# A two-layer transformer block on one core: new step orders on five engines, eleven identity products instead of thirty, new bank numbers

## The chip, the core and the metric

The kernel runs on one core of a Trainium2 chip. Five engines work side by side, each through its own list of instructions: TensorE (PE; its weight loads are shown as PEld), VectorE (DVE), ScalarE (ACT), GpSimd (POOL) and SyncE (SP), which issues DMAs. An engine takes its list strictly in order and waits on semaphores. TensorE writes into PSUM banks, VectorE and ScalarE read them, and GpSimd works in SBUF only. The metric is device time in microseconds (us).

## The reference

Two layers work on x (16 sequences of 128 tokens, 128 features) with one conditioning vector per sequence and a context of 120 tokens per sequence. Each layer is self-attention, cross-attention and an MLP, 16 heads of 8 features, all in fp32:

```
# layer 0
x_norm = ln(x) * (1 + scale_a) + shift_a;  q, k, v = x_norm @ W_qkv + b_qkv
x = x + gate_a * (softmax(q k^T * scale) v @ W_proj + b_proj)
x = x + (softmax(q_c k_c^T * scale) v_c) @ W_cproj + b_cproj     # q_c from ln(x), k_c, v_c from ln(context)
x = x + gate_m * (gelu_tanh(modulated ln(x) @ W_mlp1 + b) @ W_mlp2 + b)
# layer 1
x = x + attn(rope(q), rope(k), v) @ sa_out ;  x = x + attn(rope(q), rope(k_ctx), v_ctx) @ ca_out
x = x + gelu(adaln(x) @ ffn_w1 + b) @ ffn_w2 + b
```

## The kernel before, in words

The 16 sequences are four streams of four. A unit f (0 to 15) is one attention of one stream: 0 to 3 is the self-attention of layer 0, 4 to 7 its cross-attention, 8 to 11 the self-attention of layer 1 (with rope), 12 to 15 its cross-attention. m0 to m3 and m4 to m7 are the MLPs. A program is written by hand as five strings of step names, one for each engine (`ORDER`, line 103 on); each step becomes a few instructions, and every wait is derived from the names. Nothing moves at run time: each engine runs its string in order.

The steps of one unit, with the line of the instruction:

- `stats.f` (DVE, L592 and L595), `rstd.f` (POOL, L752 and L755), `ln.f` (DVE, L600): layer norm of the stream. `cstats`, `crstd` and `cln` do it for the context. `xT.f` (PE, L935, then ACT, L866): the transpose and the modulation. `cond`, `mods` and `vec` make the modulation vectors; `warm` is three matmuls on zeros (L975).
- `q.f`, `k.f`, `v.f` (PE, L999 and L1007). `qhi` and `khi` (ACT), `qlo` and `klo` (DVE in layer 0, POOL in layer 1) split each value into a high and a low fp32r part. In layer 1 DVE first multiplies by the cosines and sines (`q.f`, `k.f`, L618) and POOL adds (`qsum`, `ksum`).
- `khmove`, `klmove`, `qhmove`, `qlmove` (SP, L537 and L561, from unit 2 on with a clearing copy, L556): DMAs bring the parts into the row layout Ks and Qd. There are two slots, so a unit's moves wait for the last score step of the unit two before it.
- `max.f.b` (PE, L1025, 16 small matmuls into four banks, then DVE, L690, four reductions): scores of one sequence b, of which only the row maxima are kept. `mT.f.h` (PE, L1038, then ACT, L874) transposes the maxima of two sequences, `mmove.f.h` (SP, L568) brings them into Qd.
- `score.f.b` (PE, L1028, four banks, then ACT, L882, four exponentials), `value.f.b` (PE, L1058, 32 matmuls into the one bank ps_ao), `copy.f.h` (ACT, L889), `norm.f.h` (PE, L1068, then DVE, L699 and L708), `aT.f` (PE, L935, then ACT), `o.f` or `out.f` (PE), `gate` and `yT` where there is a gate, `upd.f` (DVE, L731).

The array is used in three tilings: `max` and `score` use 32 rows of it per matmul, four side by side; `value` uses column groups (18 columns per matmul); everything else the whole array. Counted over the string of PE, the tiling changes 266 times between one step and the next.

All steps but `value` take their PSUM banks from one list of seven banks (`BANK`, one digit per use); a use waits until the reader of the bank's last use has signalled (`fill`). `BESIDE` gives some steps products of the identity with itself, written into the step's own bank between that wait and the step's other wait (`keep_going`, L930).

## Time and profile before

| | us |
|---|---|
| three runs | 380.84, 383.75, 387.33 |
| median | 383.75 |
| the profiled execution | 385.06 |
| its span, first to last instruction | 383.3 |
| TensorE busy | 363.0 |
| VectorE busy | 301.7 |
| ScalarE busy | 254.5 |
| GpSimd busy | 100.6 |

### The profile page before, as it was taken

How to read it: one execution, taken by the hardware profiler on the slowest of the kernel's cores; microseconds unless marked ns; L12 is line 12 of the kernel's file. 1: busy time of each engine (PE TensorE's matmuls, PEld its weight loads, DVE VectorE, ACT ScalarE, POOL GpSimd, SP SyncE). 2: the span in 40 equal slices, each digit the busy share in tenths (PEclk: the TensorE clock that was granted, in tenths of full speed). 3: DMA queues.
4: the chain of work that ended last, by engine and by line, in shares of the span. 5: the costliest groups of instructions: out<-in, count | busy, mean ns of one | idle time of the engine just before them, and what ended most of it. 6: DMA issues, size and time to landing. Idle time of an engine off the chain costs nothing.

```text
span 383.3 us, 12514 instructions
## 1 busy us (share of the span) xinstructions
PE 363.0 (95%) x5090; PEld 260.6 (68%) x5090; DVE 301.7 (79%) x809; ACT 254.5 (66%) x513; POOL 100.6 (26%) x120
## 2 busy tenths in 40 slices
PE   7699999999999999999999999999999899999996
PEld 3485687677776776657654567666677577886776
DVE  5985989999999998947999839997799747875302
ACT  2525965578676987889453797378766945688551
POOL 6920310142020201125351234343413401031130
PEclk9966999999999999999999999999999957999999
DMA  8673244005221360014050140403140404000003
GB/s 208 259 240 93 78 140 167 9 27 186 84 88 43 127 219 5 3 32 169 2 193 6 29 168 7 169 5 106 65 168 4 168 8 159 8 3 3 2 0 111
DMA packets 19757, 34.13 MB, mean 89 GB/s; under 512 B 2740, under 2 KB 7988, under 8 KB 19700
## 3 DMA queue, kind: packets, MB, share of 16 engines
q1 hardware_dynamic: 19268, 33.24, 25.2%
q8 instruction: 41, 0.67, 0.7%
q10 hardware_dynamic: 432, 0.09, 0.2%
q14 instruction: 16, 0.13, 0.1%
HBM read 6.51 MB, written 1.05 MB: 20 GB/s over the span
## 4 chain that ended last, share of the span: by engine, by line
PE 55%; DVE 4%; ACT 3%; DMA 3%; SPq 3%; issue 2%; ACTq 0%; DVEq 0%
PE ps_ao L1058 11%; PE ps_misc L999 8%; PE ps_misc L1028 6%; PE ps_misc L1109 6%; PE ps_misc L1087 6%; PE ps_misc L1025 6%; PE ps_misc L935 3%; PE ps_misc L1094 3%; DVE maxima L690 3%; PE ps_misc L1068 2%; PE ps_misc L1007 2%; ACT PT L882 2%; DMA Ks<-Kl 2%; DMA Ks<-Kh 1%; SPq L537 1%
## 5 line engine op out<-in xcount | busy, mean ns | idle before, releaser
L690 DVE TENSOR_REDUCE maxima<-ps_misc 128x4 f32<-128x512 f32 (+1 forms) x256 | 153.5, 664 | 17.6 <-PE ps_misc L1025 17.1
L882 ACT ACTIVATE PT<-ps_misc 128x512 f32<-128x512 f32 (+1 forms) x256 | 131.7, 606 | 24.0 <-PE ps_misc L1028 22.7
L1058 PE MATMUL ps_ao<-PT,V 120*18 120x128 f32 (+1 forms) x2048 | 70.5, 282 | 0.5 <-ACT PT L882 0.5
L1025 PEld LDWEIGHTS ps_misc<-Ks,Qd 32*128 32x128 f32 x1024 | 41.9, 197 | 30.8 <-issue 11.3
L1025 PE MATMUL ps_misc<-Ks,Qd 32*128 32x128 f32 (+1 forms) x1024 | 53.4, 298 | 8.5 <-DMA Ks<-Kl 3.3
L1058 PEld LDWEIGHTS ps_ao<-PT,V 120*18 120x18 f32 (+1 forms) x2048 | 52.6, 101 | 7.4 <-issue 2.3
L1028 PEld LDWEIGHTS ps_misc<-Qd,Ks 32*128 32x128 f32 (+1 forms) x1024 | 38.0, 186 | 21.5 <-issue 13.7
L752 POOL TENSOR_SCALAR vareps<-mv 128x4 f32<-128x4 f32 (+1 forms) x28 | 6.4, 228 | 170.9 <-DVE mv L595 170.6
L1028 PE MATMUL ps_misc<-Qd,Ks 32*128 32x128 f32 (+1 forms) x1024 | 48.7, 287 | 1.5 <-DVE maxima L690 0.8
L866 ACT ACTIVATE xnT<-ps_misc,vec 128x128 f32<-128x128 f32 x80 | 30.1, 462 | 15.6 <-PE ps_misc L935 15.5
L999 PE MATMUL ps_misc<-xnT,Wr 128*128 128x512 f32 x72 | 37.5, 641 | 1.8 <-ACT xnT L866 1.6
L889 ACT ACTIVATE AOs<-ps_ao 128x512 f32<-128x512 f32 x32 | 19.3, 603 | 26.1 <-PE ps_ao L1058 26.1
L731 DVE TENSOR_TENSOR x<-ps_misc,x 128x512 f32<-128x512 f32 x24 | 16.3, 684 | 23.8 <-PE ps_misc L1109 22.8
L786 POOL TENSOR_TENSOR ropeA<-ropeA,ropeB 128x512 f32<-128x512 f32 (+1 forms) x16 | 20.0, 1257 | 50.6 <-DVE ropeB L618 50.6
L600 DVE TENSOR_SCALAR xn<-x,mv,rstd 128x128 f32<-128x128 f32 x96 | 28.3, 363 | 5.4 <-POOL rstd L755 5.4
L1087 PE MATMUL ps_misc<-xnT,W 128*128 128x512 f32 x64 | 31.1, 603 | 0.2
L755 POOL TENSOR_TENSOR rstd<-vareps,minus_half 128x4 f32<-128x4 f32 (+1 forms) x28 | 29.0, 1037 | 2.3
L911 ACT ACTIVATE hT<-ps_misc,bias 128x512 f32<-128x512 f32 x32 | 20.7, 695 | 12.1 <-PE ps_misc L1087 7.7
L592 DVE BATCH_NORM_STATS2 stats<-x 128x6 f32<-128x128 f32 x96 | 20.8, 279 | 2.9 <-DMA x<-x_in 2.4
L999 PEld LDWEIGHTS ps_misc<-xnT,Wr 128*128 128x128 f32 x72 | 12.6, 197 | 12.1 <-issue 6.5
L1068 PE MATMUL ps_misc<-cst,AOs 128*128 128x128 f32 x128 | 19.5, 280 | 1.3 <-ACT AOs L889 1.1
L1068 PEld LDWEIGHTS ps_misc<-cst,AOs 128*128 128x128 f32 x128 | 15.1, 144 | 5.9 <-issue 3.0
...
## 6 DMA issues: line engine op xcount, KB each, us to landing
...
```

Source lines behind the costliest of these rows:

```text
L600: dve.tensor_scalar(dst[0:rows, b, :], src[0:rows, b, :], mv[0:rows, which, s, b, 0:1], rstd[0:rows, which, s, b:b + 1], ALU.subtract, ALU ...
L690: dve.tensor_reduce(maxima[:, h, st.b % HB, c, :], bank(use + c)[:, 0:NG * ns].rearrange("p (n k) -> p n k", n=NG), AX_X, ALU.max, negate= ...
L755: pool.tensor_tensor(rstd[0:rows, which, st.s, :], vareps[0:rows, which, st.s, :], minus_half[0:rows, :], ALU.pow).then_inc(S["rstd_ready" ...
L866: act.activation(dst[:, b * P:(b + 1) * P], src[:, b * P:(b + 1) * P], ACT.Identity, scale=vec[:, c, mult:mult + 1], bias=vec[:, c, shift: ...
L882: act.activation(PT[0:ns, k % PSLOTS, c, :, :].rearrange("p n t -> p (n t)"), bank(use + c)[0:ns, :], ACT.Exp, scale=SCALE).then_inc(S["pr ...
L999: pe.matmul(bank(st.use + i)[:, 0:n], w_rows(f"{st.kind}{st.a}{form}"), src[:, 0:n], start=True, stop=True).then_inc(S["misc_filled"], 1)
L1025: ins = pe.matmul(bank(st.use + c)[:, n * ns:(n + 1) * ns], queries, keys, start=True, stop=True)
L1028: ins = pe.matmul(bank(st.use + c)[0:ns, n * P:(n + 1) * P], keys, queries, start=True, stop=True)
L1058: last = pe.matmul(ps_ao[32 * c:32 * c + PAIR, block * P:(block + 1) * P], heads[:, at:at + PAIR], PT[0:ns, k % PSLOTS, c, n, :], start=no ...
L1068: last = pe.transpose(bank(st.use)[:, b * P:(b + 1) * P], AOs[:, k % 2, b * P:(b + 1) * P], ident)
L1087: pe.matmul(bank(st.use), w(f"w1_{st.a}", st.b), src, start=True, stop=True).then_inc(S["misc_filled"], 1)
L1109: last = pe.matmul(bank(st.use)[:, b * D:(b + 1) * D], src[:, b * P:(b + 1) * P], weight, start=(i == 0), stop=(i == len(parts) - 1))
```

## The change

All five strings of `ORDER` and the list `BANK` are replaced. The steps are the same, none is added or dropped; what each step computes is the same. `BESIDE` has 11 entries of one product each instead of 22 entries with 30 products. Counted in the new string of PE, the tiling changes 251 times. The code of `keep_going` can now write more than four copies, and `max` and `score` could take identity products too; neither is used by the new table.

```
 BESIDE = {
-    "xT.0": 3, "xT.1": 1, "xT.2": 1, "xT.3": 1, "mT.0.0": 1, "norm.0.1": 1, "aT.0": 1, "norm.1.1": 1, "aT.1": 1,
-    "o.1": 1, "yT.1": 1, "mT.3.0": 2, "norm.3.1": 2, "aT.3": 1, "norm.8.0": 2, "norm.9.1": 1, "xT.12": 3,
-    "mT.11.0": 1, "mT.12.1": 1, "norm.12.1": 1, "norm.13.0": 1, "aT.13": 2,
+    "xT.3": 1, "mT.0.1": 1, "mT.1.0": 1, "mT.1.1": 1, "norm.2.0": 1, "norm.4.0": 1, "yT.3": 1, "mT.12.0": 1,
+    "mT.12.1": 1, "norm.12.1": 1, "mT.14.1": 1,
 }
 ORDER = {
     "pe": """
-        warm.0 mods.0 xT.0 k.0 q.0 xT.1 mods.1 q.1 k.1 max.0.0 v.0 max.0.1 v.1 max.0.2 xT.2 mT.0.0 xT.3 max.0.3 k.2
+        mods.0 warm.0 xT.0 mods.1 q.0 k.0 xT.1 v.0 xT.2 k.1 q.1 max.0.0 max.0.1 v.1 xT.3 max.0.2 v.2 mT.0.0 k.2
...
                 def keep_going(st):
                     n = BESIDE.get(st.name, 0)
-                    if n:
-                        pe.matmul(bank(st.use)[:, 0:n * P], ident, ident[:, None, :].to_broadcast([P, n, P]),
-                                  start=True, stop=True)
+                    while n:
+                        copies = min(n, CB)
+                        pe.matmul(bank(st.use)[:, 0:copies * P], ident,
+                                  ident[:, None, :].to_broadcast([P, copies, P]), start=True, stop=True)
+                        n -= copies
...
                     elif st.kind in ("max", "score"):
                         ns = ns_of(st)
+                        taken = st.name in BESIDE
+                        if taken:
+                            for c in range(HG):
+                                fill(st.use + c)
+                            keep_going(st)
...
-                                if n == 0:
+                                if n == 0 and not taken:
                                     fill(st.use + c)
```

First place: VectorE at the start of the program, before the change, from the statistics of the first stream (`stats.0`) to the second normalisation (`ln.1`).

```order
L592 BN_STATS stats<-x 128x6 x4
L595 BN_AGGR mv<-stats 128x2 x4
L655 TENSOR_SCALAR silu<-silu 128x16
L657 RECIPROCAL silu<-silu 128x16
L659 TENSOR_TENSOR silu<-hT,silu 128x16
L600 TENSOR_SCALAR xn<-x,mv,rstd 128x128 x4
L636 TENSOR_SCALAR vec<-ps_misc,bias 128x16 x2
L592 BN_STATS stats<-x 128x6 x4
L595 BN_AGGR mv<-stats 128x2 x4
L592 BN_STATS stats<-x 128x6 x4
L595 BN_AGGR mv<-stats 128x2 x4
L600 TENSOR_SCALAR xn<-x,mv,rstd 128x128 x4
```

The same place in the change, from the end of `cond`; line numbers are one lower.

```order
L591 BN_STATS stats<-x 128x6 x4
L594 BN_AGGR mv<-stats 128x2 x4
L591 BN_STATS stats<-x 128x6 x4
L594 BN_AGGR mv<-stats 128x2 x4
L635 TENSOR_SCALAR vec<-ps_misc,bias 128x16 x2
L591 BN_STATS stats<-x 128x6 x4
L594 BN_AGGR mv<-stats 128x2 x4
L599 TENSOR_SCALAR xn<-x,mv,rstd 128x128 x4
L591 BN_STATS stats<-x 128x6 x4
L594 BN_AGGR mv<-stats 128x2 x4
L591 BN_STATS stats<-craw 120x6 x4
L594 BN_AGGR mv<-stats 120x2 x4
```

The first normalisation (L600, now L599) stood behind one set of statistics and stands behind three, the third of them on stream 3; two sets of context statistics, which stood behind the first `max` steps of unit 1, follow it.

Second place: TensorE before the change, from `score.12.3` to `max.14.0`, the stretch in which the keys and queries of unit 14 have to arrive (L1028 `score`, L1058 `value`, L1025 `max`, L935 `xT.15`, L1068 `norm.12.0`, L1038 `mT.13.1`, L999 `q.15`).

```order
L1028 MATMUL ps_misc<-Qd,Ks 120x128 x16
L1058 MATMUL ps_ao<-PT,V 18x128 x16
L1025 MATMUL ps_misc<-Ks,Qd 128x120 x16
L935 MATMUL ps_misc<-cst,xn 128x128 x4
L1068 MATMUL ps_misc<-cst,AOs 128x128 x4
L1058 MATMUL ps_ao<-PT,V 18x128 x16
L1028 MATMUL ps_misc<-Qd,Ks 120x128 x16
L1038 MATMUL ps_misc<-cst,maxima 32x128
L999 MATMUL ps_misc<-xnT,Wr 128x512 x2
L1028 MATMUL ps_misc<-Qd,Ks 120x128 x16
L1025 MATMUL ps_misc<-Ks,Qd 128x120 x16
```

The same stretch in the change, from the step behind `score.12.3` on.

```order
L1044 MATMUL ps_misc<-cst,maxima 32x128
L1000 MATMUL ps_misc<-xnT,Wr 128x512 x2
L1031 MATMUL ps_misc<-Ks,Qd 128x120 x16
L936 MATMUL ps_misc<-cst,xn 128x128 x4
L1064 MATMUL ps_ao<-PT,V 18x128 x16
L1031 MATMUL ps_misc<-Ks,Qd 128x120 x16
L1064 MATMUL ps_ao<-PT,V 18x128 x16
L1034 MATMUL ps_misc<-Qd,Ks 120x128 x32
L1044 MATMUL ps_misc<-cst,maxima 32x128
L1074 MATMUL ps_misc<-cst,AOs 128x128 x4
L1000 MATMUL ps_misc<-xnT,Wr 128x512 x2
L1064 MATMUL ps_ao<-PT,V 18x128 x16
```

`q.14`, one more `max`, `mT.13.0` and a third `value` now stand between the two, and two `score` steps follow each other (L1034 x32), so there is one change of tiling less there.

Third place: SyncE in the change, from the last move of unit 14 (`klmove.14`) to the last move of unit 15 (`qlmove.15`).

```order
L536 DMA Ks<-Kl 32x4x480
L567 DMA Qd<-maxT 4x4x128 x2
L536 DMA Ks<-Kl 32x4x480
L555 DMA Qd<-no_shift 4x4x512
L560 DMA Qd<-Qh 32x4x512 x2
L567 DMA Qd<-maxT 4x4x128 x2
L536 DMA Ks<-Kh 32x4x480 x2
L560 DMA Qd<-Ql 32x4x512
```

In the change the maxima of `mmove.14.0` stand inside the moves of unit 15, in front of the two high key moves; before, they stood there too, but behind all three key moves.

## Rows read from the trace of the kernel before

**Rows 1.** The page, its parts 1 and 2: TensorE, and the granted clock in 40 slices.

```profile
PE 363.0 (95%) x5090; PEld 260.6 (68%) x5090; DVE 301.7 (79%) x809; ACT 254.5 (66%) x513; POOL 100.6 (26%) x120
PEclk9966999999999999999999999999999957999999
```

**Rows 2.** Busy time by stretch: start:end, length, engines with instruction counts, granted clock, DMA share, GB/s.

```profile
0.00:19.27 19.27, 13.98 (x52) 8.05 (x52) 14.26 (x65) 7.16 (x14) 14.62 (x20) 1.00 0.74 232
19.27:35.10 15.83, 15.53 (x115) 11.51 (x116) 10.87 (x20) 5.58 (x13) 2.31 (x3) 0.57 0.63 198
35.10:130.54 95.44, 91.10 (x1564) 68.63 (x1560) 88.89 (x240) 68.53 (x139) 16.17 (x28) 1.00 0.27 96
130.54:286.81 156.27, 151.69 (x2116) 102.65 (x2115) 132.51 (x340) 112.41 (x223) 48.70 (x50) 1.00 0.24 83
```

**Rows 3.** The same view around the late stretch of low clock, and one early stretch.

```profile
34.87:48.52 13.65, 12.25 (x210) 8.94 (x214) 12.58 (x39) 11.23 (x23) 3.69 (x8) 1.00 0.21 69
...
294.28:307.93 13.65, 11.23 (x222) 8.30 (x220) 9.96 (x28) 12.27 (x27) 6.25 (x6) 1.00 0.34 119
307.93:321.59 13.66, 13.66 (x205) 10.48 (x209) 8.22 (x16) 5.51 (x11) 1.26 (x1) 0.50 0.20 75
```

**Rows 4.** Timeline of TensorE, value.12.3 to score.13.2: start, length, instructions, [idle before, releaser].

```profile
300.49 1.07 PE L1058 MATMUL ps_ao<-PT,V 120*18 120x128 f32 x32
301.49 0.64 PE L1028 MATMUL ps_misc<-Qd,Ks 32*120 32x128 f32 x16
...
302.18 1.90 PE L999 MATMUL ps_misc<-xnT,Wr 128*128 128x512 f32 x4
304.01 0.70 PE L1028 MATMUL ps_misc<-Qd,Ks 32*120 32x128 f32 x16
306.42 0.67 PE L1025 MATMUL ps_misc<-Ks,Qd 32*128 32x120 f32 x16 [1.71 <-DMA Ks<-Kh]
...
307.86 0.44 PE L1028 MATMUL ps_misc<-Qd,Ks 32*120 32x128 f32 x4 [0.68 <-DVE maxima L690]
```

**Rows 5.** Timeline of TensorE, one value step between others.

```profile
151.04 1.07 PE L1058 MATMUL ps_ao<-PT,V 120*18 120x128 f32 x32
152.04 0.66 PE L1025 MATMUL ps_misc<-Ks,Qd 32*128 32x120 f32 x16
```

**Rows 6.** Timeline of TensorE, two value steps in a row.

```profile
174.44 1.94 PE L1058 MATMUL ps_ao<-PT,V 120*18 120x128 f32 x64
176.31 0.64 PE L1028 MATMUL ps_misc<-Qd,Ks 32*120 32x128 f32 x16
```

**Rows 7.** Timeline of TensorE: mT.12.0, score.11.3 and max.13.0.

```profile
277.59 0.27 PE L1038 MATMUL ps_misc<-cst,maxima 128*32 128x128 f32 x1 [0.38 <-DVE maxima L690]
...
278.77 0.67 PE L1028 MATMUL ps_misc<-Qd,Ks 32*128 32x128 f32 x16
...
286.81 0.66 PE L1025 MATMUL ps_misc<-Ks,Qd 32*128 32x120 f32 x16
```

**Rows 8.** Timeline of SyncE: first and last of unit 13's seven moves.

```profile
279.61 0.55 SPq L556 DMA_DIRECT2D Qd<-no_shift  x1
...
283.03 1.26 SPq L537 DMA_DIRECT2D Ks<-Kh  x2
```

**Rows 9.** Waits of TensorE: who waited for whom: us in total, times, longest.

```profile
PE ps_misc L1068 <- ACT AOs L889: 1.1, 5, 0.3
```

**Rows 10.** Timeline of VectorE at the start: stats.0, ln.0, stats.2.

```profile
3.94 0.87 DVE L592 BATCH_NORM_STATS2 stats<-x 128x6 f32<-128x128 f32 x4 [1.96 <-DMA x<-x_in]
...
6.79 1.29 DVE L600 TENSOR_SCALAR xn<-x,mv,rstd 128x128 f32<-128x128 f32 x4 [1.01 <-POOL rstd L755]
...
10.00 0.87 DVE L592 BATCH_NORM_STATS2 stats<-x 128x6 f32<-128x128 f32 x4 [0.44 <-DMA x<-x_in]
10.90 0.38 DVE L595 BATCH_NORM_AGGREGATE mv<-stats 128x2 f32<-128x6 f32 x4
```

**Rows 11.** Timeline of TensorE: the largest identity product, in front of xT.12.

```profile
248.56 0.91 PE L930 MATMUL ps_misc<-cst 128*128 128x384 f32 x2 [0.15 <-ACT V L849]
```

More of the change, by code:

```diff
@@ L110 @@
-        cT.1 q.4 score.2.2 value.2.1 score.2.3 max.3.3 xT.5 k.5 score.3.0 q.5 norm.2.0 mT.3.1 value.2.2 value.2.3
-        score.3.1 norm.2.1 max.4.0 aT.2 v.5 max.4.1 value.3.0 score.3.2 value.3.1 max.4.2 mT.4.0 score.3.3 o.2
-        max.4.3 value.3.2 score.4.0 yT.2 value.3.3 score.4.1 mT.4.1 norm.3.0 norm.3.1 max.5.0 value.4.0 score.4.2
-        aT.3 max.5.1 value.4.1 score.4.3 o.3 max.5.2 mT.5.0 xT.6 value.4.2 max.5.3 q.6 cT.2 yT.3 value.4.3
-        score.5.0 mT.5.1 norm.4.0 norm.4.1 k.6 v.6 aT.4 score.5.1 value.5.0 score.5.2 cT.3 out.4 k.7 xT.7 max.6.0
@@ L120 @@
-        max.8.2 out.7 h.m2.2 h.m2.0 h.m2.3 max.8.3 h2.m2 mT.8.0 xT.m3 max.9.0 yT.m2 h.m3.3 h.m3.1 max.9.1 mT.8.1
-        h.m3.2 h.m3.0 max.9.2 h2.m3 xT.10 mT.9.0 score.8.0 yT.m3 q.10 k.10 score.8.1 v.10 max.9.3 xT.11 value.8.0
-        score.8.2 value.8.1 score.8.3 mT.9.1 q.11 norm.8.0 score.9.0 value.8.2 score.9.1 k.11 max.10.0 value.8.3
-        score.9.2 norm.8.1 max.10.1 value.9.0 aT.8 max.10.2 value.9.1 score.9.3 norm.9.0 out.8 k.12 max.10.3
-        value.9.2 value.9.3 norm.9.1 max.11.0 v.11 mT.10.0 aT.9 xT.12 max.11.1 mT.10.1 out.9 score.10.0 q.12
@@ L130 @@
-        mT.13.1 q.15 score.13.1 max.14.0 score.13.2 value.13.0 max.14.1 value.13.1 score.13.3 norm.12.1 max.14.2
-        mT.14.0 value.13.2 max.14.3 value.13.3 score.14.0 norm.13.0 score.14.1 mT.14.1 norm.13.1 v.15 max.15.0
-        aT.12 value.14.0 max.15.1 value.14.1 score.14.2 out.12 max.15.2 mT.15.0 score.14.3 aT.13 max.15.3
-        value.14.2 score.15.0 value.14.3 score.15.1 mT.15.1 out.13 xT.m4 norm.14.1 norm.14.0 value.15.0 score.15.2
-        value.15.1 score.15.3 h.m4.2 aT.14 h.m4.3 xT.m5 out.14 norm.15.0 value.15.2 value.15.3 h.m5.0 norm.15.1
@@ new lines @@
+        yT.1 q.4 mT.3.0 score.2.3 value.2.2 max.3.2 cT.1 value.2.3 norm.2.0 max.3.3 v.5 xT.5 score.3.0 q.5 max.4.0
+        mT.3.1 norm.2.1 k.5 score.3.1 value.3.0 aT.2 max.4.1 value.3.1 score.3.2 max.4.2 mT.4.0 cT.2 o.2 score.3.3
+        value.3.2 max.4.3 value.3.3 score.4.0 yT.2 k.6 score.4.1 norm.3.0 v.6 norm.3.1 cT.3 mT.4.1 value.4.0
+        max.5.0 max.5.1 aT.3 value.4.1 o.3 score.4.2 score.4.3 max.5.2 value.4.2 mT.5.0 xT.6 max.5.3 value.4.3 q.6
+        norm.4.1 norm.4.0 score.5.0 mT.5.1 yT.3 aT.4 score.5.1 out.4 value.5.0 score.5.2 score.5.3 value.5.1 k.7
@@ new lines @@
+        xT.7 max.6.0 xT.m0 value.5.2 max.6.1 value.5.3 max.6.2 v.7 norm.5.1 q.7 mT.6.0 h.m0.1 norm.5.0 h.m0.2
+        h.m0.0 aT.5 max.6.3 h.m0.3 out.5 score.6.0 mT.6.1 h2.m0 score.6.1 value.6.0 xT.m1 max.7.0 value.6.1
+        score.6.2 h.m1.2 yT.m0 max.7.1 h.m1.1 h.m1.3 h.m1.0 mT.7.0 max.7.2 value.6.2 score.6.3 h2.m1 xT.8 max.7.3
+        value.6.3 score.7.0 yT.m1 k.8 norm.6.1 mT.7.1 value.7.0 score.7.1 norm.6.0 q.8 aT.6 value.7.1 score.7.2
+        out.6 v.8 xT.9 norm.7.0 value.7.2 score.7.3 k.9 q.9 xT.m2 max.8.0 value.7.3 max.8.1 h.m2.3 norm.7.1 h.m2.1
@@ new lines @@
+        h.m2.2 max.8.2 aT.7 h.m2.0 out.7 v.9 max.8.3 mT.8.0 h2.m2 max.9.0 xT.m3 max.9.1 mT.8.1 h.m3.0 h.m3.3 h.m3.2
+        max.9.2 mT.9.0 h.m3.1 score.8.0 yT.m2 h2.m3 score.8.1 value.8.0 max.9.3 yT.m3 xT.10 value.8.1 score.8.2
+        mT.9.1 q.10 v.10 norm.8.0 score.8.3 k.10 xT.11 value.8.2 value.8.3 score.9.0 score.9.1 q.11 norm.8.1 k.11
+        score.9.2 max.10.0 max.10.1 aT.8 value.9.0 out.8 score.9.3 value.9.1 max.10.2 mT.10.0 v.12 norm.9.0
+        value.9.2 value.9.3 max.10.3 v.11 norm.9.1 k.12 score.10.0 aT.9 max.11.0 mT.10.1 xT.12 out.9 max.11.1
@@ new lines @@
+        value.10.0 score.10.1 k.13 q.12 score.10.2 max.11.2 value.10.1 score.10.3 value.10.2 max.11.3 mT.11.0
+        norm.10.0 xT.13 v.13 value.10.3 mT.11.1 q.13 score.11.0 score.11.1 norm.10.1 k.14 score.11.2 max.12.0
+        value.11.0 max.12.1 value.11.1 aT.10 max.12.2 mT.12.0 out.10 score.11.3 norm.11.0 value.11.2 max.12.3
+        value.11.3 v.14 norm.11.1 k.15 score.12.0 aT.11 xT.14 max.13.0 mT.12.1 out.11 score.12.1 max.13.1
+        value.12.0 score.12.2 value.12.1 score.12.3 mT.13.0 q.14 max.13.2 xT.15 value.12.2 max.13.3 value.12.3
@@ new lines @@
+        score.13.0 score.13.1 mT.13.1 norm.12.0 q.15 value.13.0 max.14.0 score.13.2 max.14.1 value.13.1 score.13.3
+        norm.12.1 max.14.2 mT.14.0 aT.12 value.13.2 max.14.3 value.13.3 score.14.0 norm.13.0 v.15 mT.14.1 max.15.0
+        score.14.1 out.12 max.15.1 value.14.0 score.14.2 norm.13.1 max.15.2 mT.15.0 value.14.1 score.14.3 aT.13
+        value.14.2 max.15.3 value.14.3 score.15.0 score.15.1 mT.15.1 out.13 norm.14.1 xT.m4 norm.14.0 value.15.0
+        value.15.1 score.15.2 score.15.3 aT.14 h.m4.2 xT.m5 out.14 h.m4.0 norm.15.0 value.15.2 value.15.3 h.m4.1
```

142 lines of the change are left out of this document (66 added, 76 removed).

## The prediction

> **What bounds the kernel now.** I read the page first: TensorE is busy 363 of 383 us, so its queue looks like the bound, but the clock row drops below 9 in two places, early and in the slices at about 308 us [rows 1]. Next the stretches. Up to 19.27 us, where the first `max` step starts, VectorE is busy 14.3 us; from there to 35.1 the clock averages 0.57 and VectorE is idle 5.0 us. From 35 to 131 us VectorE is busy 88.9 of 95.4 us (93%), so TensorE partly waits for the maxima it must hand over. From 131 to 287 us TensorE is busy 151.7 of 156.3 us and bounds alone [rows 2]. Then comes a stretch in which TensorE is idle 2.4 us, and behind it 13.7 us at clock 0.50, with TensorE busy all the time [rows 3].
>
> The timeline shows what stood behind that idle time: `max.14.0` waited 1.71 us for a key move, and `score.13.2` stopped 0.68 us in the middle for VectorE's maxima [rows 4]. The same rows give lengths without a wait, from start to start: a value step 1.00 us, a rope query 1.83 us.
>
> I also summed such lengths over all 415 steps, in both orders. Before, TensorE needs about 316 us at full clock; the other 64 us up to its last matmul are waits, start and low clock. A change of order can only reach these 64 us, and the changes of tiling inside the 316.
>
> **The change, part by part.** The steps are the same, so only their places have a price.
>
> *Tiling.* 266 changes become 251, 15 fewer. A value step between steps of other tilings takes 1.00 us [rows 5]; two in a row take 1.87 us, not 2.00 [rows 6]. The one change saved is worth 0.13 us: 15 x 0.13 = **-2.0 us**. All of it lies on TensorE's own queue; where VectorE is the bound it may be lost, so -1.0 to -2.0. The Trainium skill says in TensorEngine Tiling (Array Packing), Key Properties, that switching the tiling mode drains TensorE, and in TensorE: Matmul & The Clock Gate, Step-by-step, that a drain is about 128 cycles; an estimate from these two would be 0.05 us a change at 2.4 GHz and 0.8 us in all. By the rows it is more than twice that, and I go by the rows.
>
> *Moves of keys and queries.* They share two slots, so a unit's seven moves start when the last score of the unit two before is done. For unit 13 that was at 279.44 (278.77 + 0.67), and `max.13.0` started at 286.81: 7.4 us [rows 7]. It is seven issues in 4.68 us, 0.67 each, and 2.5 us from the last issue to the start [rows 8]. Where TensorE has less than 7.4 us of other steps in between, it waits. Summed from step lengths, it had 6.4, 6.1, 6.8 and 7.2 us before units 10 to 13, which makes 1.0 + 1.3 + 0.6 + 0.2, and unit 14 cost the 2.4 us of [rows 4]: 5.5 us together. In the change the same sums are 9.8, 9.8, 10.3 and 7.8 for units 10 to 13: no wait. What is late next are units 14 and 15. For 14, `q.14` now stands directly behind `score.12.3`, and VectorE, GpSimd, ScalarE and SyncE each have a step between it and `max.14.0`; TensorE has 10.1 us behind the score but only 8.1 us behind the query. The price is between 0 and the 2.4 us of [rows 4]; I take 1.5. For 15, the maxima moves of `mmove.14.0` stand inside the seven moves: nine issues, 9 x 0.67 + 2.5 = 8.5 us, against 6.4 us of steps: 2.1 us. Behind `max.15.0` queue `mT.15.0` and with it all of the last unit. Net: -5.5 + 1.5 + 2.1 = **-1.9 us** (bounds -5.5 to +1).
>
> *The late low clock.* 13.66 us at half speed with TensorE busy throughout [rows 3] cost half of that, 6.8 us. In the change the two waits of 1.5 and 2.1 us lie over 10 us apart with steps between them, where before 1.71 and 0.68 us followed within 1.5 us [rows 4]. An early stretch in which TensorE was idle 1.4 us was followed by full clock [rows 3]. I take the fall as gone: **-6.8 us** (bounds -6.8 and 0).
>
> *Waits for copies of the sums.* Five `norm` steps waited for ScalarE's copy, 1.1 us in all [rows 9]: they stood right behind one step after the last value. In the new order every `norm` has at least 0.86 us of steps in front of it: **-1.1 us**.
>
> *Waits for maxima.* `mT.12.0` waited 0.38 us with 2.0 us of steps behind the last `max` [rows 7]. Before, three `mT` steps stood that close (2.03 or less); in the change five do, with 2.03 to 2.12: two more at 0.38, **+0.8 us** (bounds 0 and 2).
>
> *The start.* The first normalisation ran at 6.79 us, after one set of statistics. Now it stands behind `stats.1` and `stats.3`. The third block of x that VectorE took was waited for until 10.00 [rows 10], and stream 3 is loaded about as late, one 240 KB context block earlier; I take its statistics to end at 10.7, so `ln.0` moves 3.9 us. From there to the low part of the first keys VectorE has two sets of statistics of x and of context more than it had (1.28 us each [rows 10]), two more normalisations and the long `vec.1`. Adding its steps gives `klo.0` at about 21 us and the first `max` at 24 to 25 us against 19.27. What comes back: up to `max.2.0`, at 55 us, VectorE has the same list of work in both orders, and before it was idle 5.0 + 5.0 us up to 35.1 [rows 2], waiting for x, then for a slow TensorE. In the new order I count 7.6 us of such idle time up to the first `max`, and little after it, since the work there no longer has to fit between matmuls at half clock. Between 2.4 us gained and the full 4.8 us lost I take **-0.6 us**. On GpSimd, `crstd.2` now waits for context statistics that VectorE does much later, and `rows1` (weights for units 4 to 7) is queued behind it; these are used a stream later, so I put nothing for it.
>
> *Identity products.* 19 fewer; three took 0.91 us [rows 11], about 0.3 each, so 0 to -5.8 us. They stand in front of a wait of their own step, which goes on without them: I take 0.
>
> *Banks.* New numbers move waits between readers; I have no row that prices one by itself, so they sit in the range.
>
> Sum: -2.0 - 1.9 - 6.8 - 1.1 + 0.8 - 0.6 = -11.6 us, from the profiled execution's 385.1 us: **373.5 us**. That execution is 1.3 us above the median of 383.75; the three runs spread from 380.8 to 387.3, so I leave that difference in the range.
>
> **The rivals.**
>
> *The low clock comes back somewhere.* For it: 19 products less are standing in waits between 35 and 131 us, where TensorE's own steps fill little over three quarters of the time by my sums, and units 14 and 15 still wait. Against it: the waits are split. It costs the 6.8 us again: 380.3 us.
>
> *The waits only move.* The first half stays bound by VectorE, whose work there only shrinks by what moved to the start, and in the second half places that were loose have become tight: maxima to transposes from 5.3 to 3.8 us at unit 6, 8.9 to 2.6 at unit 7. The change then does not do what it says, and only tiling is left: 385.1 - 2.0 = 383 us.
>
> *The start is lost and not given back; slower.* The first normalisation waits for stream 3, `max.0.0` starts 4.8 us later, TensorE stands idle in that time, and a second stretch at 0.5 follows the first, in which all units 0 and 1 run at half speed. Price 4.8 + 6.8, with the late fall staying: 385.1 - 2.0 + 11.6 = 394.7 us. It decides if the first `max` starts after 26 us. For it speaks that x arrives when the DMA queue lets it, against it VectorE's 5 us of idle time behind it.
>
> **How the numbers follow.** Forecast 0.50, low clock again 0.24, waits only move 0.16, start lost 0.10. Two per cent of 383.75 is 7.7 us, about what a measurement of this kernel can tell from no change; faster is below 376.1, slower above 391.4. Of the forecast some 0.05 lies above 376.1, since the start alone is uncertain by 5 us; faster 0.45, same 0.05 + 0.24 + 0.16 = 0.45, slower 0.10. The forecast's own range is 368 to 378 (start, banks and identity products). To leave out no more than 0.2 I go up to 387, which takes in the second case and most of the third: 368 to 387.
>
> **What would show it.** Right: one low stretch of the clock, the early one; no key wait before `max.10.0` to `max.13.0`; 1 to 2 us of it before `max.14.0` and `max.15.0`; no `norm` waiting for its copy; the first `max` near 24 us, `max.2.0` near 55 us again. Wrong: clock 0.50 in a second stretch; `max.2.0` after 58 us; VectorE less busy than 93% in the first half; or single long waits for PSUM banks on TensorE that this page does not have.

## The result, and the profile after

The change made the kernel slower: 425.35 us (median of 4 runs, 418.59 to 428.36) against 383.40 us (4 runs, 380.84 to 387.33); the ratio is 1.1012, 95% interval 1.0817 to 1.1207. The medians are over all runs; each ratio in this document is over the faster of two groups into which a kernel's executions fall, here 418.59 and 423.94 us of the four, so it is not the quotient of the medians. The forecast was 373.5 us, the range 368 to 387.

Two numbers of each run split the 42 us: the span and TensorE's mean granted clock. Their product is the span counted in TensorE's granted cycles and written as us at full clock; I call it the **index**. It is not a time, since only TensorE slows with the clock. It moves less between runs of one kernel than the time does: 388.5 to 393.0 in the four runs after, mean 390.4, and 370 to 372 as the mean of the runs of the kernel before in every comparison below. It is not quite free of the clock: it is lowest where the clock is lowest (388.5 at 0.911 and 393.0 at 0.943 after; 367.8 at 0.955 and 374.1 at 0.990 before), so a few us of index between kernels of different clock say little. Some 20 us of the 42 are index, nearly all of it waiting. The clock itself was 0.91 to 0.94 after (mean 0.924) and about 0.97 before: that is the other half.

The page after, parts 1 and 2, against [rows 1]:

```profile
PE 375.9 (90%) x5068; PEld 266.6 (64%) x5068; DVE 304.8 (73%) x809; ACT 254.7 (61%) x513; POOL 100.8 (24%) x120
PEclk9977997999999999999999996996899986989999
```

TensorE is busy 12.9 us more, and it is idle 416.8 - 375.9 = 40.9 us where it was idle 383.3 - 363.0 = 20.3. The other engines do what they did. The clock row has not one dip behind the start but a string of them.

The stretches of [rows 2], cut at the same steps (`max.0.0`, `max.1.0`, `max.6.0`, `max.13.0`); columns as there:

```profile
0.00:23.83 23.83, 13.52 (x58) 8.45 (x58) 18.42 (x83) 8.82 (x19) 18.46 (x24) 1.00 0.59 181
23.83:40.27 16.44, 14.99 (x109) 10.41 (x110) 12.33 (x20) 5.27 (x12) 0.00 (x0) 0.69 0.60 184
40.27:145.97 105.70, 94.47 (x1588) 69.11 (x1587) 86.82 (x232) 69.15 (x140) 16.11 (x28) 0.97 0.25 89
145.97:316.18 170.21, 161.75 (x2074) 108.66 (x2074) 131.64 (x330) 110.32 (x219) 47.79 (x49) 0.95 0.22 76
```

4.6 us are lost up to `max.0.0`, 0.6 in the second stretch, 10.3 in the third and 13.9 in the fourth, which TensorE had filled. VectorE falls from 93% to 82% in the third: it did not become the bound there. What took its place stands in the list of waits. TensorE's waits at `max` (L1025) and `score` (L1028) for ScalarE's exps, and those of its matmul queue (PE) for VectorE's maxima, before (us in total, times, longest):

```profile
PEld ps_misc L1025 <- ACT PT L882: 3.7, 11, 0.8
PEld ps_misc L1028 <- ACT PT L882: 3.0, 8, 0.8
PE ps_misc L1025 <- ACT PT L882: 1.2, 4, 0.7
PE ps_misc L1028 <- ACT PT L882: 0.3, 2, 0.2
PE ps_misc L1028 <- DVE maxima L690: 0.8, 2, 0.7
PE ps_misc L1025 <- DVE maxima L690: 0.3, 1, 0.3
```

and after, where the lines are L1031 and L1034:

```profile
PEld ps_misc L1031 <- ACT PT L881: 10.1, 26, 0.9
PEld ps_misc L1034 <- ACT PT L881: 9.5, 16, 0.9
PE ps_misc L1034 <- ACT PT L881: 6.8, 13, 0.7
PE ps_misc L1031 <- ACT PT L881: 5.8, 18, 0.7
PE ps_misc L1031 <- DVE maxima L689: 3.7, 10, 0.7
PE ps_misc L1034 <- DVE maxima L689: 1.7, 5, 0.7
```

For the exps 8.2 us in 25 waits became 32.2 in 73. That counts the weight loads (PEld) too, whose waits run beside those of the matmuls; the matmuls alone waited 1.5 us in 6 before and 12.6 in 31 after, and for maxima 1.1 us in 3 and 5.4 in 15. Over all its lines TensorE's matmul queue waits 2.2 us before and 17.0 after for exps, 1.5 and 5.8 for maxima; with the 7.8 us before its first step (shown at e12), these are most of the 40.9 us idle. Exps and maxima read PSUM, so at `max` and `score` these are steps that wait for a bank. One place shows how such a wait comes about and what follows. Timeline of TensorE after, `o.0`, `score.1.2`, `score.1.3`, `max.2.2`, `value.1.2`:

```profile
63.19 1.12 PE L1087 MATMUL ps_misc<-attT,W 128*128 128x512 f32 x2
64.25 0.77 PE L1034 MATMUL ps_misc<-Qd,Ks 32*128 32x128 f32 x17
65.75 0.32 PE L1034 MATMUL ps_misc<-Qd,Ks 32*128 32x128 f32 x1 [0.74 <-ACT PT L881]
66.24 0.66 PE L1034 MATMUL ps_misc<-Qd,Ks 32*128 32x128 f32 x14 [0.17 <-ACT PT L881]
66.73 2.09 PE L1031 MATMUL ps_misc<-Ks,Qd 32*128 32x128 f32 x16
68.75 1.91 PE L1064 MATMUL ps_ao<-PT,V 128*18 128x128 f32 x32
```

ScalarE in the same stretch:

```profile
65.10 4.03 ACT L881 ACTIVATE PT<-ps_misc 128x512 f32<-128x512 f32 x8 [1.18 <-PE ps_misc L1034]
```

The 17 matmuls at 64.25 are all of `score.1.2` and one of `score.1.3`. Each step takes four of the seven banks, so the second must write banks that ScalarE has yet to read: it waits 0.74 us for the first exp and 0.17 for the next. ScalarE's eight exps take 4.03 us, the two steps' matmuls 1.0. The order after has 22 such pairs of four-bank steps, the order before 7. And the granted clock around it (same columns as above):

```profile
60.00:66.83 6.83, 5.43 (x95) 3.66 (x91) 6.57 (x15) 3.57 (x8) 0.00 (x0) 1.00 0.00 1
66.83:73.66 6.83, 6.72 (x99) 4.78 (x97) 5.13 (x14) 2.30 (x5) 4.49 (x8) 0.50 0.57 199
```

The clock drops to 0.50 right behind those waits, with TensorE busy from then on: `value.1.2` takes 1.91 us instead of 1.07 [rows 5]. Such waits are not followed by a fall every time. In the stretch below TensorE was idle 1.61 us, where it was idle 1.40 in the first of the two above, and the clock stayed at 1.00 until 251 us:

```profile
121.47:128.30 6.83, 5.22 (x101) 3.46 (x93) 5.94 (x13) 2.84 (x7) 3.66 (x6) 1.00 0.02 5
```

After the change the clock is at 0.50 in eight stretches, 47.8 us together; before, in two of 13.7 us.

### The profile page after: what moved, and what is told of

The parts are those of the page before. It is cut to its first block, busy times and chain, and to the rows that moved or that the text cites. A ratio compares the mean times of both kernels' runs of the same rounds, so it can differ in the third digit from the quotient of the medians.

```text
span 416.8 us, 12480 instructions
## 1 busy us (share of the span) xinstructions
PE 375.9 (90%) x5068; PEld 266.6 (64%) x5068; DVE 304.8 (73%) x809; ACT 254.7 (61%) x513; POOL 100.8 (24%) x120
## 4 chain that ended last, share of the span: by engine, by line
PE 60%; ACT 9%; DVE 6%; issue 3%; SPq 1%; DMA 1%; ACTq 0%
PE ps_ao L1064 11%; PE ps_misc L1034 8%; PE ps_misc L1000 8%; ACT PT L881 8%; PE ps_misc L1031 7%; PE ps_misc L1115 6%; PE ps_misc L1093 6%; DVE maxima L689 5%; PE ps_misc L1100 3%; PE ps_misc L936 3%; PE ps_misc L1074 3%; PE ps_misc L1008 2%; PE ps_misc L1044 1%; DMA Ks<-Kl 1%; PE ps_misc L1087 0%
## 5 line engine op out<-in xcount | busy, mean ns | idle before, releaser
L1064 PE MATMUL ps_ao<-PT,V 120*18 120x128 f32 (+1 forms) x2048 | 71.9, 285 | 1.3 <-ACT PT L881 0.7
L1031 PE MATMUL ps_misc<-Ks,Qd 32*128 32x128 f32 (+1 forms) x1024 | 59.2, 302 | 13.4 <-ACT PT L881 5.8
L1031 PEld LDWEIGHTS ps_misc<-Ks,Qd 32*128 32x128 f32 x1024 | 45.3, 199 | 36.0 <-issue 11.3
L1034 PEld LDWEIGHTS ps_misc<-Qd,Ks 32*128 32x128 f32 (+1 forms) x1024 | 40.2, 190 | 33.7 <-issue 17.4
L1034 PE MATMUL ps_misc<-Qd,Ks 32*128 32x128 f32 (+1 forms) x1024 | 51.9, 291 | 9.3 <-ACT PT L881 6.8
L865 ACT ACTIVATE xnT<-ps_misc,vec 128x128 f32<-128x128 f32 x80 | 30.4, 474 | 20.3 <-PE ps_misc L936 20.3
L599 DVE TENSOR_SCALAR xn<-x,mv,rstd 128x128 f32<-128x128 f32 x96 | 28.5, 363 | 7.2 <-POOL rstd L754 7.2
L910 ACT ACTIVATE hT<-ps_misc,bias 128x512 f32<-128x512 f32 x32 | 20.8, 690 | 10.7 <-PE ps_misc L1093 10.6
L1074 PE MATMUL ps_misc<-cst,AOs 128*128 128x128 f32 x128 | 21.6, 297 | 0.5 <-ACT AOs L888 0.5
L1074 PEld LDWEIGHTS ps_misc<-cst,AOs 128*128 128x128 f32 x128 | 16.1, 152 | 5.8 <-issue 3.5
```

The lines of the kernel that those rows point to most:

```text
L599: dve.tensor_scalar(dst[0:rows, b, :], src[0:rows, b, :], mv[0:rows, which, s, b, 0:1], rstd[0:rows, which, s, b:b + 1], ALU.subtract, ALU ...
L865: act.activation(dst[:, b * P:(b + 1) * P], src[:, b * P:(b + 1) * P], ACT.Identity, scale=vec[:, c, mult:mult + 1], bias=vec[:, c, shift: ...
L1031: ins = pe.matmul(bank(st.use + c)[:, n * ns:(n + 1) * ns], queries, keys, start=True, stop=True)
L1034: ins = pe.matmul(bank(st.use + c)[0:ns, n * P:(n + 1) * P], keys, queries, start=True, stop=True)
L1064: last = pe.matmul(ps_ao[32 * c:32 * c + PAIR, block * P:(block + 1) * P], heads[:, at:at + PAIR], PT[0:ns, k % PSLOTS, c, n, :], start=no ...
L1074: last = pe.transpose(bank(st.use)[:, b * P:(b + 1) * P], AOs[:, k % 2, b * P:(b + 1) * P], ident)
```

## The experiments

Theories: **A**, four-bank steps side by side wait for banks; **B**, fewer identity products let the clock fall; **C**, the start; **D**, badly chosen bank numbers. All runs in one table: "idle" is the profiled run's span minus TensorE's busy time, the ratio is to the kernel before and stands where an interval is on record. The mean clock and the index are over all runs of a kernel, the idle time is of one. e12 is a single run.

| kernel | median us | ratio (95%) | mean clock | index | idle us |
|---|---|---|---|---|---|
| before | 382 to 384 | | 0.97 | 370 to 372 | 20.3 |
| e10 before, short exps | 376.1 | 0.984 (0.976-0.991) | 0.977 | 366.7 | 22.5 |
| e14 less waiting | 390.2 | 1.020 (1.013-1.026) | 0.966 | 375.8 | 24.1 |
| e4 before, 11 products | 391.0 | | 0.953 | 369.7 | 24.4 |
| e16 less waiting, memsets minded, second | 391.7 | 1.021 (1.006-1.036) | 0.970 | 378.0 | 24.7 |
| e3 before, 15 pairs joined | 398.6 | 1.039 (1.032-1.045) | 0.966 | 383.5 | 26.4 |
| e15 less waiting, memsets minded | 394.1 | 1.029 (1.014-1.044) | 0.965 | 377.8 | 26.6 |
| e5 after, start of before | 410.6 | 1.071 (1.062-1.081) | 0.939 | 383.7 | 30.8 |
| e13 before, six banks | 431.9 | 1.125 (1.115-1.136) | 0.929 | 400.5 | 30.9 |
| e6 before, start of after | 402.1 | 1.046 (1.035-1.056) | 0.948 | 379.1 | 32.2 |
| e7 after, split and new banks | 409.9 | 1.076 (1.068-1.084) | 0.949 | 385.6 | 32.9 |
| e2 after, new banks | 420.1 | | 0.927 | 387.2 | 33.8 |
| e9 after, short exps | 395.6 | 1.037 (1.031-1.044) | 0.958 | 377.8 | 33.8 |
| e12 after, memset later | 424.0 | | 0.918 | 387.6 | 37.5 |
| e8 after, 30 products | 429.6 | 1.121 (1.111-1.131) | 0.922 | 394.0 | 40.2 |
| e11 after, warm-up first | 426.9 | 1.118 (1.107-1.129) | 0.908 | 386.8 | 40.8 |
| after | 425.4 | 1.101 (1.082-1.121) | 0.924 | 390.4 | 40.9 |
| e1 after, pairs split | 431.6 | 1.120 (1.109-1.130) | 0.906 | 390.1 | 42.2 |

**e1, pairs split.** 20 of the 22 pairs pulled apart in TensorE's order by one step, such as

```
-  max.0.0 max.0.1 v.1          -  score.5.2 score.5.3 value.5.1     -  value.15.1 score.15.2 score.15.3
+  max.0.0 v.1 max.0.1          +  score.5.2 value.5.1 score.5.3     +  score.15.2 value.15.1 score.15.3
```

> The changed kernel with 20 of its 22 places where two four-bank steps (max, score) stand directly behind each other pulled apart by one neighbouring step; the same bank numbers stay with the same steps; tiling changes go from 251 to 279. Theory A (neighbouring four-bank steps wait for banks): the 22 second steps carry 28.9 us of time beyond their own length in the trace of the changed kernel, the 20 about 25; minus 28 x 0.13 = 3.6 us of tiling: 400 to 407 us, and the waits of TensorE for exps and maxima at max and score fall to about the figures of the kernel before. Theory D (the bank numbers as such are badly chosen, wherever the steps stand): the numbers are the same, so most of the waits stay: 415 us or more. Theory B (fewer identity products let the clock fall): the products are the same, the stretches at 0.5 stay near 48 us: 415 us or more. Theory C (the start): the first max stays near 24 us and no more than the 4.8 us lost there can come from it: unchanged.

Measured: 431.6 us, index 390.1. The named waits for exps at `max` and `score` fell from 32.2 to 11.1 us, those for maxima stayed (18.6 and 19.1), and the idle time did not fall at all: `v`, `o` and `xT` now wait for banks, since each step had kept its numbers. A in its simple form (400 to 407 us) gains nothing. 431.6 us lies in the "415 us or more" of B and D, though B's stretches at 0.5 did not stay near 48 us (71.7); they are decided by e2, e4 and e8.

**e2, new bank numbers.** Only the digits of `BANK` differ.

> The changed kernel with its orders kept and only the list of bank numbers replaced: each use takes the bank whose last reader was done earliest in the trace of the changed kernel. Theory D: most of the 42 us that it lost comes back: 385 to 400 us. Theory A: two steps that take 4 of 7 banks each must share one whatever the numbers; only the 11 steps that share two or three banks with the step right in front gain, 0.4 us each (1.46 against 1.06 on the average): 418 to 423 us. Theories B and C: no change, 422 to 428 us.

Index 387.2, 3.2 less; median 420.1. As A said (418 to 423): D is worth some 3 us of index and 5 of the median, not 42.

**e3, pairs joined in the kernel before.** 15 edits of this kind:

```
-  max.11.3 value.10.2 score.10.3 q.13
+  max.11.3 score.10.3 value.10.2 q.13
```

> The kernel before with 15 value steps, each between two four-bank steps, moved one place behind the second, so that 22 pairs of four-bank steps adjoin instead of 7; bank numbers stay with their steps, tiling changes go from 266 to 249. Theory A: 15 pairs cost 1.06 to 1.46 us each, 16 to 22 us, minus 17 x 0.13 = 2.2 us: 397 to 403 us. Theories B, C and D: nothing of theirs is touched, only tilings are saved: 380 to 384 us.

398.6 us, index up 13, ratio 1.039. The place edited above, in the joined kernel:

```profile
269.36 0.67 PE L1025 MATMUL ps_misc<-Ks,Qd 32*128 32x128 f32 x16
269.86 0.27 PE L1028 MATMUL ps_misc<-Qd,Ks 32*128 32x128 f32 x2
270.80 0.88 PE L1028 MATMUL ps_misc<-Qd,Ks 32*128 32x128 f32 x14 [0.67 <-DVE maxima L690]
271.62 1.07 PE L1058 MATMUL ps_ao<-PT,V 128*18 128x128 f32 x32
```

`score.10.3` starts 0.50 us behind `max.11.3` and, two matmuls in, waits for the maxima. From its start to the next step's it takes 1.76 us, where before it took 0.65. 15 value steps moved by one place cost (13 + 17 x 0.13) / 15 = 1.0 us each. The price of a pair is thereby shown in the kernel before, where nothing else was changed (the 0.13 us for a tiling is the prediction's). The clock, though, stayed at 0.966.

**e4 and e8, the products.** e4 is the kernel before with the table `BESIDE` of the change, e8 the reverse.

> The kernel before with the eleven single identity products of the changed kernel instead of its 30. Theory B: the clock falls for longer, by up to the 20 us at 0.5 that the changed kernel has more, so plus 5 to 10 us: 388 to 394 us. Theory A: the low stretches come from TensorE's waits, so the clock stays as it was and 19 products less give 0 to 5.8 us: 378 to 384 us.

> The changed kernel with the 30 identity products of the kernel before (at the steps of the same names) instead of its eleven. Theory B: the granted clock rises from 0.92 towards the 0.966 of the kernel before and 10 to 20 us come back: 405 to 415 us, with span times clock unchanged at 388 to 394 us. If products cost TensorE time, span times clock rises by up to 19 x 0.3 = 5.7 us. If the low clock comes from the waits alone, 420 to 428 us.

e4: index 369.7, clock 0.953; e8: index 394.0, clock 0.922. The products carry none of the index in e4 (my zero was right for it) and cost 3.6 us in e8; giving them back does not give the clock back (0.922 against 0.924). B falls as the cause of the 42 us. It is not refuted for the kernel before: e4's median of 391.0 lies inside B's 388 to 394 and not in A's 378 to 384. Its four runs go from 383.2 to 394.3 us at clocks of 0.972 to 0.938, beside 0.966 for the kernel before; whether the missing products cost some us of clock there stays open.

**e5 and e6, the start exchanged.** In all five queues the order of one kernel up to `max.4.2`, of the other behind it, with its banks and products.

> The changed kernel with the order of the kernel before in all five queues up to max.4.2 (the first 99 TensorE steps, the same set in both orders; 98.5 us into the kernel before, 107.4 us into the changed one), with its banks and products there; behind it everything as in the changed kernel. Theory C (the start): what is lost up to there, 107.4 - 98.5 = 8.9 us, comes back, some 5 us of it at full clock: span times granted clock falls from 390 to 383 to 386 us. Theory A (four-bank steps side by side): of the 22 pairs 17 stand behind that place, and the two kernels have 5 each up to there: span times clock stays at 380 to 386 us, not near the 370 of the kernel before. If the start were the main cause, it would come down to 375 us or less.

> The mirror of it: the kernel before with the order of the changed kernel in all five queues up to max.4.2, and its own order, banks and products behind it (7 pairs in all). Theory C: plus 5 us of span times clock from the start and no more: 375 to 378 us against 370; and the low clock of the changed kernel in its first 107 us. Theory A: the same number, since the later 17 pairs are missing. Both together say that e5 and e6 share the 20 us of span times clock in the proportion of about 5 to 15.

Index 383.7, which is 6.7 below the change and 12.0 above the kernel before beside it, and 379.1, which is 7.4 above it. The start costs a little more than C's 375 to 378 said. The two losses add up: some 7 us of index in the start, 11 to 12 behind it.

**e7, pairs split, and banks chosen for that order.** The edits of e1 and new digits.

> The changed kernel with 20 of 22 pairs of four-bank steps pulled apart (as in e1) and bank numbers chosen anew for that order, each use taking the bank that comes free first. In e1 the steps were apart, but their banks were still those of the old places, and span times clock did not fall (387 to 393 us). Theory A with that excuse: the pairs' waits go now, minus 25 us plus 28 x 0.13 = 3.6 us, to 370 to 375 us of span times clock. Theory A2 (it is not the neighbourhood as such: the new order asks for more banks in a short time than seven can serve, and a value step between does not cure that): no lower than 380 us. Median time 395 to 410 us by A, 410 to 425 by A2.

Index 385.6, 381.4 to 391.5 in its four runs, ratio 1.076: A2 by the index; the median of 409.9 us would fit A's 395 to 410 as well. Against e2 the split is worth 1.6 us, 5 before its own 28 tiling changes. So a step between does not cure a pair here, and the 1.0 us that a pair cost in e3 does not come back. One reason may be that a value step is 1.0 us of cover where ScalarE needs 2.0 us for a step's four exps (the rows above: 4.03 us for eight). It is not shown: in the profiled run, whose index is the 391.5, the matmul queue's waits for exps are down to 3.3 us (17.0 after the change, 2.2 before) and those for maxima are 5.8 as after, yet it is idle 32.9 us. What else keeps e7 some 14 us above the kernel before, beyond the start, stays open.

**e9 and e10, short exps.** Both kernels with

```
+  heads = NG if k < PSLOTS else 1
-  act.activation(PT[0:ns, k % PSLOTS, c, :, :]...,       bank(use + c)[0:ns, :], ...)
+  act.activation(PT[0:ns, k % PSLOTS, c, 0:heads, :]..., bank(use + c)[0:ns, 0:heads * P], ...)
```

> The changed kernel with ScalarE's exps cut to the first 128 of 512 columns from the fourth score step on (what it leaves out: three quarters of the probabilities, which keep older values; every matmul, wait and order stays). A bank of a score step then comes free after one short exp instead of 0.48 us, a whole step after less than half of 1.9 us. Theory A2 (the orders ask for banks faster than their readers hand them back, and ScalarE's exps are the reader that TensorE waits for most in this trace: 32 us named at max and score against 8 us before): span times clock falls by 15 to 20 us, from 390 to 370 to 375, and with it TensorE's idle time, and so the granted clock comes up to 0.95 or more: 385 to 400 us. If the loss lay in tilings, the start, moves or VectorE alone, it falls by no more than the 5 us of its twin e10.

> The same cut of the exps (the first 128 of 512 columns from the fourth score step on) in the kernel before: the twin of e9. Theory A2: here TensorE waits for exps only 8 us in all as the page sums them, so 3 to 6 us: span times clock 365 to 368, median 372 to 380 us; the distance of e9 to e10 is then the 7 to 8 us of the start instead of 20. If the exps cost both kernels the same, the distance stays 20 us.

The exps' row of e9; a mean of 298 ns, where the full ones take 606:

```profile
L882 ACT ACTIVATE PT<-ps_misc 120x128 f32<-120x128 f32 (+2 forms) x256 | 54.0, 298 | 78.2 <-PE ps_misc L1035 77.9
```

The index falls by 12.6 us after and by 3.5 before: the distance between the orders shrinks from 20 to 11. Somewhat short of the 15 to 20, and the 11 are more than the 7 to 8 that A2 left for the start, but far from equal: the new order hangs on how long the exps take, the old one hardly. Short exps hand banks back sooner, and they also free ScalarE for its other steps, 256 exps by 0.3 us each; the two were not separated.

**e11, warm-up first.** `mods.0 warm.0` becomes `warm.0 mods.0` in TensorE's order.

> The changed kernel with its first two TensorE steps changed back: warm.0 before mods.0, so that TensorE starts at about 1.4 instead of 7.8 us. Theory C2 (the cold start of TensorE is what sets the clock low early): the stretch at 0.5 that begins at 26 us shortens or goes and the rest stays: 415 to 422 us. Theory E (the clock falls with TensorE's idle time summed over the whole run, 38 us against 17 us before): the idle time behind 8 us is the same, the clock stays at 0.91 to 0.93: 421 to 428 us. Span times clock is the same in both, 388 to 393 us.

426.9 us, clock 0.908, a shade below E's 0.91: the cold start is not it.

**e13, six banks.** The kernel before with other digits in `BANK`, 0 to 5.

> The kernel before, same orders in all queues, same 30 products, with six banks instead of seven (each use takes the one of six that comes free first; the seventh is only written by the warm-up). It makes TensorE wait more without any change of order. Theory A2 (banks are what the order lives on): every one of 128 four-bank steps now shares at least two banks with the four-bank step in front of it; at 0.1 to 0.4 us for each that is 13 to 50 us of span times clock more, 383 to 420. Theory E (the granted clock falls with TensorE's idle time, whatever the reason for it): idle time rises by as much, and the clock falls from 0.97 to 0.93 or lower, so that the time rises by about twice the waits: 410 us or more. Rival to E (it is something in the new orders, their start for instance, that sets the clock): clock stays at 0.96 to 0.98.

Index 400.5, 29.5 more; clock 0.929 where the runs beside it had 0.973; 431.9 us. Order, start and products are those of the kernel before, so **waits alone lower the clock** here, and one bank fewer costs more index than the whole change. Idle time rose by only 10.6 us in the profiled run (30.9 against 20.3), so it does not hold all the waiting. The page of that run, the longest of the four (440.8 us):

```profile
PE 408.1 (93%) x5090; PEld 286.5 (65%) x5090; DVE 305.8 (70%) x809; ACT 257.0 (59%) x513; POOL 100.8 (23%) x120
PEclk9957686998886999999999999999999955869999
```

**e12, GpSimd's memset later** (one run).

```
-  fix0 fixV rstd.0 rows0 rstd.1 fix1
+  fix0 rstd.0 rows0 fixV rstd.1 fix1
```

> The changed kernel with GpSimd's fixV (its memset of V, 2.98 us) moved from in front of rstd.0 to behind rstd.0 and rows0. In the changed kernel VectorE's first operation of cond, 128x16, takes 2.92 us, from 4.33 to 7.25, while that memset runs from 4.24 to 7.22; in the kernel before the same operation takes 0.14 us. Theory P (the two engines hold each other up): it takes about 0.15 us again, mods.0 starts at about 5 instead of 7.80 us. Rival (it waits for its data, silu, or for its own first use): it stays near 2.9 us and mods.0 at 7.8. The whole time is not expected to change by more than 3 us, since fixV now stands in front of rstd.1.

After the change, VectorE's first operation of `cond`, GpSimd's memset of V, and the first TensorE step:

```profile
4.24 2.98 POOL L761 MEMSET V<- 128x3456 f32 x1
4.33 2.92 DVE L654 TENSOR_SCALAR silu<-silu 128x16 f32<-128x16 f32 x1 [2.35 <-ACT silu L816]
...
7.80 1.03 PE L945 MATMUL ps_misc<-silu,hT 128*128 128x16 f32 x4 [7.80 <-DVE silu L658]
```

In e12, with `ln.0` as well:

```profile
4.38 0.17 DVE L654 TENSOR_SCALAR silu<-silu 128x16 f32<-128x16 f32 x1 [2.41 <-ACT silu L816]
5.28 1.00 PE L945 MATMUL ps_misc<-silu,hT 128*128 128x16 f32 x4 [5.28 <-DMA hT<-weights]
...
8.42 2.98 POOL L761 MEMSET V<- 128x3456 f32 x1
9.89 2.20 DVE L599 TENSOR_SCALAR xn<-x,mv,rstd 128x128 f32<-128x128 f32 x4
```

The operation takes 0.17 us again, and the memset now holds `ln.0` until it ends at 11.40: 2.20 us where four such normalisations take 1.09 elsewhere. GpSimd's memset does hold VectorE's operation up. The whole run took 424.0 us, so nothing came of it for the total. The Trainium skill has a rule for this in SBUF — State Buffer, Who interferes with whom: GpSimd's ports are one of VectorE's two pairs, a tensor_scalar can run in a mode that takes that shared pair too, and whichever instruction issues first keeps it until it ends. Both rows agree with it: the memset starts first, at 4.24 before 4.33 and at 8.42 before 9.89, and the operation ends behind it.

**e14, less waiting.** Many single steps of the kernel before moved in all five queues, and the bank numbers chosen anew; for one (VectorE):

```
-  ln.1 klo.0 qlo.0 stats.3 ln.2
+  ln.1 ln.2 klo.0 qlo.0 stats.3
```

> The kernel before with single steps moved by a few places in its queues (96 of 415 TensorE places differ, no step passes one of its own kind) and banks chosen anew, wherever step lengths and reader times summed from the trace of the kernel before leave TensorE waiting less; 9 pairs of four-bank steps, 263 tiling changes. The sums say 3 us of waits less. Theory E (waits cost about twice, the second time by the clock): span times clock 367 to 368 against 370 to 371, median 374 to 380 us. Rival (the sums are no better than those by which the change was made: an order that is tight on paper loses on the chip): 383 us or more.

390.2 us, index 375.8, 4.5 above the kernel before: the rival. One place where it went wrong is again in the start:

```profile
13.05 2.97 POOL L761 MEMSET V<- 128x3456 f32 x1
13.12 5.29 DVE L599 TENSOR_SCALAR xn<-x,mv,rstd 128x128 f32<-128x128 f32 x4 [0.42 <-POOL rstd L754]
16.08 0.48 POOL L763 MEMSET V<- 128x192 f32 x1
16.40 1.87 POOL L766 MEMSET Ks<- 128x2048 f32 x1
```

A normalisation put in front of two `klo`/`qlo` steps met three memsets and took 5.29 us instead of 1.09. The sums by which the order was made had no row for that.

**e15 and e16, the same with the memsets minded.** Two more orders, made with that row, again with new bank numbers.

```
   e14, VectorE:  ... ln.1 ln.2 klo.0 qlo.0 stats.3 ...
   e15, VectorE:  ... ln.1 klo.0 stats.3 qlo.0 ln.2 ...
```

> Made like e14 from the step lengths of the kernel before, but with one more row in the sums: a normalisation, or the first operation of cond, waits while GpSimd runs one of its memsets, as e12 and e14 show; klo.0 and stats.3 therefore stand in front of qlo.0 and ln.2 again, as in the kernel before. 106 of 415 TensorE places differ from it, 8 pairs, 267 tiling changes; the sums say 3.6 us of waits less than before. If the memset was what e14 lacked: index 367 to 369 against 370 to 371, its 5.29 us normalisation back to about 1.1, and 374 to 381 us in the median. If an order that is tight by such sums loses for other reasons too: index 373 or more, 385 us or more.

> A second order made in the same way from another starting point (106 TensorE places differ from the kernel before, 10 pairs, 265 tiling changes; the sums say 3.3 us of waits less than before), so that the answer does not hang on one order. The same two expectations as for e15: index 367 to 369 and 374 to 381 us, or 373 or more and 385 us or more.

394.1 and 391.7 us, index 378: the second expectation, twice. In e15 `ln.2` takes 1.11 us again, so the memset was real and was not all. Three orders that save 3 us in sums over the rows of one trace lose 4 to 7 us of index on the chip. In time they lose 2 to 3%, with intervals that reach from 0.6 to 4.4%, and how much of it is the new orders and how much the new bank numbers was not tested. In e15 two steps that looked free wait longest, `max.1.0` and `max.6.0`:

```profile
36.37 0.68 PE L1025 MATMUL ps_misc<-Ks,Qd 32*128 32x128 f32 x16 [1.25 <-issue]
133.07 0.67 PE L1025 MATMUL ps_misc<-Ks,Qd 32*128 32x120 f32 x16 [1.88 <-issue]
```

The trace names no releaser there, so what they waited for stays open. No run that computes the whole result beats the kernel before.

## Why the prediction was wrong, by its own steps

*Banks: the step that failed.* "New numbers move waits between readers; I have no row that prices one by itself, so they sit in the range." In the sum they stood at nothing. It was not the numbers (e2: 3 us) but the order that made TensorE wait for the readers of its banks: 17.0 us for exps and 5.8 for maxima on its matmul queue, where it was 2.2 and 1.5, and with short exps the index falls by 12.6 after and 3.5 before (e9, e10). The plainest trait of that order is 22 instead of 7 pairs of four-bank steps side by side, and there was a row with a price for these. The last line of [rows 4] is such a pair: `score.13.2` directly behind `max.14.0`, stopped 0.68 us after two matmuls by VectorE's maxima. I read it as part of the story of one low clock. Counted as a price, 15 more pairs would have made some 10 us; measured, a pair costs 1.0 us with its step (e3). It is also where saved tilings came from: a `max` behind a `score` needs no change of tiling, so in e3 each 0.13 us gained was bought with 1.0. The pairs are not the whole of it: 20 of them pulled apart, with banks to match, give back 5 us (e7 against e2), so which other traits of the order make TensorE wait stays open.

*The late low clock.* "I take the fall as gone": behind the early stretch there were seven more at 0.50, 37.6 us together, where before there was one of 13.7. I had weighed where single waits lie against each other, and taken from [rows 3] that 1.4 us idle in a stretch did no harm; 1.40 us between 60.00 and 66.83 stood before a fall. From kernel to kernel the mean clock goes roughly with TensorE's idle time as a whole: above 40 us idle it was 0.906 to 0.924, below 27 it was 0.953 to 0.977, in between 0.918 to 0.958, and e13 shows waits lowering it with nothing else changed. Single runs scatter more: profiled runs idle for 31 to 33 us had clocks from 0.903 (e13) to 0.979 (e7). Which waits count, by length or place, stays open: e3's 13 us of index more came with a clock of 0.966.

*The start.* `max.0.0` came at 23.83, just short of the forecast 24 to 25. That it is given back was wrong: `max.2.0` came at 59.52, past the 58 that the prediction had set as its own limit, and e5 and e6 put the loss at some 7 us of index. The third rival, the lost start, had the right place and sign; with its 394.7 us it was still 31 short, since it counted no waits for banks and of the clock only one more stretch. Nor was x what `ln.0` waited for: after the change VectorE takes stream 3 at 10.29 us without a wait for x, in e12 at 8.69. Part of the delay was that GpSimd's memset stood in front of `rstd.0` and held up `cond`: `ln.0` starts at 11.48 after the change, at 9.89 in e12.

*Tiling.* No run changes the tilings alone, so the -2.0 is neither borne out nor refuted; beside 42 us it is small.

*Moves of keys.* No wait for them before units 11 to 15, and 0.23 us before `max.10.0`, where I had put 1.5 and 2.1 us for units 14 and 15: better than forecast, and of no use, since `max.10.0`, `max.12.0` and `max.13.0` wait for exps instead (0.74 us in one piece at `max.12.0`). The bound of +1 in that paragraph is not the sum of its own terms, which give -1.0 at the most; nothing hung on it.

*Copies, maxima, products.* One `norm` waits for its copy, 0.5 us, instead of five for 1.1; one `mT` for maxima, 0.2 us. Products at nothing: right for the index (e4), open for the clock in the kernel before.

*VectorE "less busy than 93%" and "single long waits for PSUM banks"* were named as what would show the forecast wrong, beside a second stretch at 0.50 and a late `max.2.0`. All but the long waits happened: no wait of TensorE's matmuls for exps or maxima at `max` and `score` is longer than 0.7 us on the lists above, before or after. It was the number of short ones that rose.

What adds up to the 20 us of index: the start 7 (e5, e6), the rest behind it, of which the length of ScalarE's exps makes 9 between e9 and e10. These overlap and were not taken apart further. The other half is the clock: 390.4 / 0.924 = 422.5 us of span against 390.4 / 0.97 = 402.5.
